# Weight maxima reduced by TensorE in place of GpSimd, and the first two turns of a fused recurrent kernel in another order

## What is computed

```
xn = layernorm(x)                       # over the 128 channels
# layer 0
xm = xn * time_mix + shift(xn) * (1 - time_mix)
k, v, r = exp(min(xm @ Wk.T, 60)), xm @ Wv.T, xm @ Wr.T
wkv, wk = causal_conv(k * v, w), causal_conv(k, w) + 1e-9   # w: exponential decay + a factor for the present
s = (sigmoid(r) * wkv / wk) @ Wo.T
h = relu(s0 * [xn, -xn] @ sign(k0)) * 2;  h = relu(s1 * h @ sign(k1)) * 2;  g = silu(s2 * h @ sign(k2))
x = x + s * g
# layer 1: a state-space block for s, a mixture of 2 shared and 16 routed experts for g
x = x + s * g
```

## Time and profile before

| | us |
|---|---|
| median of three runs (lowest, highest) | 738.07 (735.55, 738.98) |
| the profiled execution | 734.49 |
| its span | 732.7 |
| TensorE busy in the span | 642.5 (88%) |
| VectorE busy | 635.7 (87%) |
| ScalarE busy | 509.4 (70%) |
| GpSimd busy | 281.5 (38%) |

### The profile page before, as it was taken

One profiled execution on the slowest core, in us unless ns is written; L12 is line 12 of the kernel. 1 busy time (PEld: TensorE's weight loads), 2 busy tenths in 40 slices (PEclk: granted clock), 3 DMA queues, 4 the chain that ended last, 5 costly groups with the idle time before them and its releaser, 6 DMA issues. The chain is left out here.

```text
span 732.7 us, 10841 instructions
## 1 busy us (share of the span) xinstructions
PE 642.5 (88%) x2711; PEld 304.7 (42%) x2711; DVE 635.7 (87%) x1467; ACT 509.4 (70%) x800; POOL 281.5 (38%) x278
## 2 busy tenths in 40 slices
PE   2795899999999985598999899999999999999986
PEld 1342444444444442343444444444444444544432
DVE  4996999999999997758988988988898898889766
ACT  2463566766666652687877887787788779788775
POOL 6456666777767762031222123032212303221220
PEclk9898999999999997899999999999999999999999
DMA  5420000000000000000000000000000000000000
GB/s 151 110 90 26 0 0 0 0 0 0 0 0 0 1 0 1 0 1 0 15 1 15 15 0 14 14 14 0 14 14 0 14 14 14 0 14 14 1 16 29
DMA packets 10739, 11.29 MB, mean 15 GB/s; under 512 B 4800, under 2 KB 6288, under 8 KB 10720
## 3 DMA queue, kind: packets, MB, share of 16 engines
q1 hardware_dynamic: 9744, 10.73, 4.8%
q0 software_dynamic: 112, 0.33, 0.2%
q10 hardware_dynamic: 864, 0.00, 0.1%
HBM read 6.87 MB, written 4.19 MB: 15 GB/s over the span
## 5 line engine op out<-in xcount | busy, mean ns | idle before, releaser
L1058 PE MATMUL bank<-arena,w 128*128 128x512 f16 x640 | 153.9, 389 | 20.0 <-DVE arena L717 14.1
L1058 PE MATMUL bank<-arena,dnT 128*128 128x512 f32 x288 | 138.6, 592 | 0.0
L613 ACT ACTIVATE arena<-bank,xinv 128x512 f32<-128x512 f32 x144 | 95.6, 687 | 51.0 <-PE bank L1058 50.8
L443 POOL TENSOR_TENSOR arena<-arena 128x512 f32<-128x512 f32 x48 | 59.7, 1271 | 151.8 <-ACT arena L550 151.8
L1058 PEld LDWEIGHTS bank<-arena,w 128*128 128x128 f16 x640 | 63.4, 100 | 99.0 <-issue 24.5
L476 ACT ACTIVATE arena<-bank 128x512 f16<-128x512 f32 x96 | 53.9, 606 | 35.1 <-PE bank L1058 35.1
L433 POOL TENSOR_TENSOR arena<-arena 128x512 f32<-128x512 f32 x16 | 17.1, 1067 | 150.5 <-DVE arena L917 150.5
L1058 PE MATMUL bank<-arena,wsqT 128*128 128x512 f32 x128 | 65.6, 617 | 6.0 <-DVE arena L726 6.0
L1058 PEld LDWEIGHTS bank<-arena,dnT 128*128 128x128 f32 x288 | 53.7, 191 | 36.0 <-issue 24.3
L926 DVE SCALAR_TENSOR_TENSOR arena<-bank,cws,arena 128x506 f32<-128x506 f32 (+1 forms) x96 | 67.1, 740 | 1.1
L717 DVE SCALAR_TENSOR_TENSOR arena<-bank,arena 128x512 f16<-128x512 f32 x96 | 60.2, 670 | 1.7 <-ACT arena L476 0.5
(11 more groups left out here) (208 smaller groups left out, 1525.3 us busy)
## 6 DMA issues: line engine op xcount, KB each, us to landing
x_all<-in_L_attn_x SPq DMA_DIRECT2D x16, 256.0 KB, 2.7
out<-x_all SPq DMA_DIRECT2D x16, 256.0 KB, 2.0
up_n<-in_L_ffn_routed_up SPq DMA_DIRECT2D x1, 512.0 KB, 3.8
dn_n<-in_L_ffn_routed_down SPq DMA_DIRECT2D x1, 512.0 KB, 5.4
wx<-in_L_attn_W_x SPq DMA_DIRECT2D x1, 288.0 KB, 2.8
k_u<-in_L_ffn_k POOLq DMA_DIRECT2D x1, 256.0 KB, 5.1
w_in<-in_L_attn_W_in SPq DMA_DIRECT2D x1, 256.0 KB, 2.4
k_u<-in_L_ffn_k SPq DMA_DIRECT2D x1, 128.0 KB, 5.7
```

Of the source, the lines that this page charges most:

```text
L443: g.tensor_tensor(prod[:, c, :], act[:, c + 1, :], gate[:, :], ALU.mult).then_inc(sem["b_actp"], 1)
L613: a.activation(act[:, c, :], q_U[(c + 1) % 2][:, :], ACT.Gelu, scale=xinv[:, I_UP:I_UP + 1]).then_inc(sem["b_act"], 1)
L1058: return nc.tensor.matmul(ps, lhsT, rhs, start=start, stop=stop)
```

## The change

Seven edits, all in the stretch ahead of turn 3:

1. `partition_all_reduce` on POOL is gone. In turn 1, PE transposes `amax` into the bank `b_S`, DVE takes the maximum of each of the 7 rows and multiplies the identity by it (`largest`, between its two scans), PE multiplies ones by that diagonal matrix, which puts the seven maxima into every partition, and DVE copies them back after its four low parts. PE's first s product waits for that copy.
2. `scales` runs after turn 1 in place of after turn 2.
3. Group 0's rows are normalised by DVE (four instructions) and no longer by POOL (two).
4. DVE forms `w0` and the sign constants after `xm` of turn 0, and the decays after the four low parts of turn 0, which now stand ahead of the scans. ACT's four high parts of turn 0 stand behind the exponential, and its small constants behind `xh`.
5. The turned squares are made in two halves (two banks), and ACT takes them out.
6. PE waits for Wk and Wv alone before its first work; k0 is loaded third, Wr and Wo behind it, each with a semaphore of its own. ACT's small loads have three semaphores in place of one.
7. POOL's clearing of buffers comes two instructions earlier, and with it SyncE's loads of layer 1's weights.

```diff
-            for i in range(4):
-                last = nc.tensor.transpose(b_S[:, i * P:(i + 1) * P], wsq[:, i, :], ident[:, :])
-            last.then_inc(sem["square_turned"], 1)
+            def square_turned(half):
+                for i in range(2):
+                    last = nc.tensor.transpose((b_S, b_F)[half][:, i * P:(i + 1) * P], wsq[:, 2 * half + i, :], ident[:, :])
+                last.then_inc(sem["square_turned"], 1)
+            square_turned(0)
...
-            def constants():
-                pool.wait_ge(sem["absmax_ready"], NSC)
-                g.partition_all_reduce(amax[:, :], amax[:, :], P, bass.bass_isa.ReduceOp.max).then_inc(sem["absmax_all"], 1)
-            bodies(pool, layer0, {1: constants, G - 1: lambda: spread_of_rows(0)})
+            bodies(pool, layer0, {G - 1: lambda: spread_of_rows(0, "b_")})
...
-            normalise(0, "a_")
+            spread_of_rows(0, "a_")
...
+                if isinstance(f, int) and f == 1:
+                    pe.wait_ge(sem["absmax_ready"], NSC)
+                    pe.wait_ge(sem["square_ready"], 1)
+                    nc.tensor.transpose(b_S[0:NSC, 0:P], amax[:, :], ident[:, :]).then_inc(sem["absmax_turned"], 1)
...
+                if isinstance(f, int) and f == 1:
+                    pe.wait_ge(sem["absmax_diag"], 1)
+                    mm(b_S[:, P:P + NSC], ones[0:NSC, :], adiag[0:NSC, :]).then_inc(sem["absmax_spread"], 1)
...
+                    if isinstance(m, int) and m == 0:
+                        pe.wait_ge(sem["absmax_all"], 1)
...
+            normalised(0, "a_")
...
+            def largest():
+                dve.wait_ge(sem["absmax_turned"], 1)
+                link(v.tensor_reduce(amx[0:NSC, :], b_S[0:NSC, 0:P], AX.X, ALU.max))
+                v.tensor_scalar(adiag[0:NSC, :], ident[0:NSC, 0:NSC], amx[0:NSC, 0:1], None,
+                                ALU.mult).then_inc(sem["absmax_diag"], 1)
...
+                if isinstance(f, int) and f == 1:
+                    dve.wait_ge(sem["absmax_spread"], 1)
+                    v.tensor_copy(amax[:, :], b_S[:, P:P + NSC]).then_inc(sem["absmax_all"], 1)
...
-            bodies(dve, layer0, {0: magnitudes, 2: scales, G - 1: matrices, G: turned_matrices})
+            bodies(dve, layer0, {0: magnitudes, 1: scales, G - 1: matrices, G: turned_matrices})
```

More of the change, by code:

```diff
@@ L495, in layer0 @@
                     high(1, m, 2)
+                if isinstance(f, int) and f == 0:
+                    for j in range(FC):
+                        high(0, 0, j)
                 if has(f):
@@ L507, in layer0 @@
                     a.activation(thr[:, :], b_RX[:, :], ACT.Tanh, scale=0.5).then_inc(sem["a_thr"], 1)
-                    high(0, f, 0)
+                    if not (isinstance(f, int) and f == 0):
+                        high(0, f, 0)
                     actv.wait_ge(sem["a_thr"], f + 1)
@@ L511, in layer0 @@
                     a.activation(sr[:, :], thr[:, :], ACT.Copy, scale=0.5, bias=0.5).then_inc(sem["a_sr"], 1)
-                    high(0, f, 1)
-                    high(0, f, 2)
-                    high(0, f, 3)
+                    if not (isinstance(f, int) and f == 0):
+                        high(0, f, 1)
+                        high(0, f, 2)
+                        high(0, f, 3)
                 if has(m):
@@ L712, in _, with normalised @@
-            v.tensor_scalar(c3[:, 2:3], c3[:, 1:2], 0.5, None, ALU.mult).then_inc(sem["const_done"], 1)
+            def normalised(n, ph):
+                dve.wait_ge(sem[ph + "rstd"], n + 1)
+                after(dve, sem[ph + "xnT"], n)
+                for j in range(J):
+                    last = v.tensor_scalar(xn[:, j, :], x_all[:, bass.ds(n * N + j * P, P)], mv[:, j, 0:1],
+                                           rstd[:, j:j + 1], ALU.subtract, ALU.mult)
+                last.then_inc(sem[ph + "xn"], 1)
@@ L714, in low, with decays @@
+            def decays():
+                dve.wait_ge(sem["const_ready"], 7)
+                dve.wait_ge(sem["chan_ready"], 3)
+                dve.wait_ge(sem["const_done"], 1)
+                v.tensor_scalar(c3[:, 2:3], c3[:, 1:2], 0.5, None, ALU.mult)
+                v.tensor_scalar(dec[:, 0:P], ones[:, :], tch[:, 1:2], None, ALU.mult)
+                v.tensor_scalar(dec[:, P:T], ones[:, 0:T - P], tch[:, 1:2], None, ALU.mult).then_inc(sem["const_done"], 1)
             def low(layer, n, j):
@@ L751, in layer0 @@
                     v.tensor_tensor(kv[:, :], ekm[:, :], b_V[:, :], ALU.mult).then_inc(sem["a_kv"], 1)
+                if isinstance(f, int) and f == 0:
+                    for j in range(FC):
+                        low(0, 0, j)
+                    decays()
+                    dve.wait_ge(sem["const_done"], 2)
                 if has(m):
@@ L884, in turned_low @@
                 v.scalar_tensor_tensor((xl, xl_)[par][:, :], ps[:, :], XS, (xh, xh_)[par][:, :], ALU.mult, ALU.subtract).then_inc(sem["b_xl"], 1)
-            def normalised(n):
-                dve.wait_ge(sem["b_rstd"], n + 1)
-                after(dve, sem["b_xnT"], n)
-                for j in range(J):
-                    last = v.tensor_scalar(xn[:, j, :], x_all[:, bass.ds(n * N + j * P, P)], mv[:, j, 0:1],
-                                           rstd[:, j:j + 1], ALU.subtract, ALU.mult)
-                last.then_inc(sem["b_xn"], 1)
-            bodies(dve, layer0, {0: magnitudes, 2: scales, G - 1: matrices, G: turned_matrices})
+            bodies(dve, layer0, {0: magnitudes, 1: scales, G - 1: matrices, G: turned_matrices})
             def top_four(n):
@@ L1110, in layer0 @@
                     turn_rows(b_T).then_inc(sem["a_xnT"], 1)
+                if isinstance(f, int) and f == 0:
+                    pe.wait_ge(sem["wr_loaded"], WR_ALL)
+                    square_turned(1)
                 if has(m):
```

110 lines of the change are left out of this document (66 added, 44 removed).

## The result

The changed kernel took 729.02 us (median of four runs, 724.93 to 730.5) against 738.04 for the kernel before beside it (four runs, 735.55 to 738.98): the medians differ by 9.0 us. The ratio on record is 0.9896, with a 95% interval of 0.9867 to 0.9925, which is a gain of 7.7 us, between 5.5 and 9.8. Forecast were 726.3 and a gain of 11.8: faster, as predicted and inside the range, but by less. The profiled executions are 734.49 and 728.02, 6.5 apart; 722.7 was forecast for the second.

A forecast was written before the change was run, and what follows sets the result against it. DVE fills the loop turns; POOL's 13.33 us absence for the reduction lengthens turn 2 to 3. X = 26.6 + 15.45 + 3.5 = 45.6; gain 57.35 - 45.6 = 11.8, so 738.07 becomes 726.3 us (profiled 722.7), range 722.5 to 731.5.

The forecast's parts named there:

- The rule of the Trainium skill: At POOL's reduction: only the first call's code loading of some 6 us counts, nothing behind it; gain 4.9 us.
- D: Loop turns 2 to 14: scans beside POOL's products add 1.1 to 1.3 us per turn; 743.3 at most; chance 0.03.
- Turn 0: Start of layer 0: `xm` of turn 0 at 10.4 us, then 16.2 to `xm` of turn 1, at 26.6.
- the normalising: Ahead of `xm` of turn 0: DVE's four normalising instructions take 1.6 us, bounds 1.11 and 2.78.
- the term of turn 1: From `xm` of turn 1 to the end of `sg`: 15.45 us, where before took 16.19.
- rival B: Turn 1: PE's clock falls after idle time; k, v and two hidden blocks slow, 2.0 us less gain, 728.3; chance 0.20.
- `largest`: DVE in turn 1: the row reduction and 7x7 product take 0.5 us for both, ends 0.3 and 1.9.
- `scales`: In its new place after turn 1: 3.5 us, ends 2.4 and 5.57.
- C: Ends of turn 1 and start of turn 2: PE's waits also lower the clock; with B some 4 us more, 732.3; chance 0.10.
- each of the two waits is below 2 us: Argument against C: PE's waits in turn 1 for the diagonal and for the copy are each below 2 us.
- The rest of the kernel only moves earlier: Behind turn 4: everything keeps its length, so the gain of 11.8 us carries to the end.
- the steps apply from X on: From the start of turn 2's `xm`, X = 45.6 us: the before's steps of 15.15 and 15.53 follow to turn 4.

The follow-up runs named there:

- e7: The kernel before with the POOL reduction done twice in a row; 734.32 us (one run) against 734.09 for before.
- e1: The kernel before with edits 1 and 2 alone, its start left as before; 729.71 us against 735.47, ratio 0.9914.
- e6: The changed kernel with `scales` back after turn 2, the reduction staying on TensorE; 731.26 us (one run) against 734.09 for before.
- e4: The changed kernel with 18 overwritten products in PE's idle time ahead of k and v of turn 1; 724.36 us, ratio 0.9832 to before.
- e8: The changed kernel with POOL's two large normalising steps for group 2 behind its three products of turn 1; 725.68 us (one run) against 734.09 for before.
- e5: The changed kernel with the edits of e3 and e4 together; 724.02 us against 734.09 for before, ratio 0.9847.
- e3: The changed kernel with DVE's copy of the maxima ahead of the four low parts of turn 1; 728.03 us, ratio 0.9873 to before.
- e12: The changed kernel with the edits of e4 and e8, plus 34 overwritten products in PE's idle time between the layers; 722.41 us, ratio 0.9848 to before.
- e2: The changed kernel with the reduction back on POOL and `scales` back after turn 2; 735.08 us against 735.47 for before, ratio 0.9991.
- e9: e1 with 20 overwritten products in PE's idle time before turn 1's first hidden products; 726.72 us against 735.04 for before, ratio 0.9874.

## Why the prediction was right, and where it was wrong

**Right: what bounds and what goes.** POOL's absence of 13.33 us was the cause of the long step; without the reduction PE's 5.87 and DVE's 6.91 are gone (they stand again in e7), and by e1 the whole measured gain comes from edits 1 and 2. Which share is whose isn't shown: without edit 2 the lead at turn 4 was 3.1 (e6). The rule of the Trainium skill, GPSIMD Engine Reference, section Instruction dispatch, by itself (gain 4.9) was rightly set aside: e7 shows both idle times as a pair, and at T4 e1 gained 8.97, with the 1 us of scatter. The loop's pace is unchanged (15.53), so D, the slower rival, did not occur. Turn 0 was nearly right: 10.80 for 10.4, and 16.41 for 16.2 to turn 1. In it the normalising took 1.62 for 1.6, and neither of the bounds, 1.11 and 2.78, was near.

**Wrong: the term of turn 1.** From `xm` to the end of `sg` 15.45 were forecast, and 45.92 - 27.21 = 18.71 measured up to the start of `scales`. The 3.26 us more fall, step by step by the start times of DVE, into:

- 1.00 at the low parts (34.07 to 36.41, where 37.35 to 38.69 before): k and v at the lower clock. This is rival B, in which the forecast had put 0.20. B was priced at 2.0; e4 shows 2.65 at T4. It came in a smaller form than described: k and v lost 1.80, and the 16 hidden products behind them nothing (3.65).
- 0.80 and 0.97 at the two pairs of scans. The prediction asked for POOL's contention in turn 0 and, with D, in the loop, but took the scans of turn 1 over from before, where they had ended just as POOL began. `largest` between the pairs puts the second one onto POOL's work (e1, e4), the wait ahead of them also the first. e8, with POOL's order alone changed, brings both back.
- 0.35 at `largest` (0.85 for 0.5, inside the bounds of 0.3 and 1.9), and 0.39 at the end: s took 1.10 and came later behind the copy, so DVE waited 0.77, not 0.33. Small terms give 0.25 back.

**Wrong, and in its favour: `scales`.** 3.5 were forecast, with 2.4 as the lower end; it took 1.95, with all 16 instructions at 0.12 to 0.23. The lower end, 5.57 less four times 0.8, took off too little. e5 and e6 show the same list at 3.52 and 4.46 as soon as POOL works beside it.

**C came in part.** Behind the wait of 2.44 us ahead of s the granted clock fell (0.50 from 46 to 48), and the next 8 hidden products took 3.38. That is the 16.15 us step from turn 2 to 3 where 15.15 was taken over from before: 1.00 more. Against it stood "each of the two waits is below 2 us"; one was longer. C's price of 4 was too high; e3, in which this wait is gone, has the full clock there and a step of 15.10.

**Not in the sum: what comes behind.** "The rest of the kernel only moves earlier" was wrong. 8.49 us at T4 became 6.58 at the second normalised rows of layer 1 (307.15 - 300.57) and 6.5 at the end of the profiled pair. That the start of layer 1 can meet a lower clock wasn't thought of. Whether it does so because it comes earlier, or for something in this stretch, stays open: e12 wins 2.2 us there ahead of the `w_in` products and leaves these at the lower clock, so it doesn't show why nine unlike kernels fall in the same group.

**How the number came inside the range.** In part by errors that cancel. `xm` of turn 2 came 2.3 late: 0.6 from the start and 3.3 from turn 1, less 1.6 won in `scales`. The step to turn 3 added 1.0 and the stretch between the layers 1.9, together 5.2 of the 5.3 us by which the profiled execution, 728.02, missed 722.7. The range held the median of 729.02 because it had been drawn wide enough for B.

**Edits costed at nothing.** Edits 3 to 7 are worth 2.9 to 3.2 us at turn 0 and 1.4 at turn 1. At turn 4 they are worth 2.3 where the reduction stays on POOL (e2 against before), but -0.5 (e1 against after) or 0.4 (e9 against e4) with edits 1 and 2, nothing beside the scatter. That they would be kept was the unspoken part of "the steps apply from X on"; in the changed kernel PE stands still for 3.95 us ahead of k and v, with its clock down behind it, and with PE kept busy in both most of the lead goes all the same: where it goes then wasn't followed.

## What to carry to other kernels

In this kernel a custom instruction of GpSimd of 0.40 us kept its engine away for 13.33. Such a one is priced by how long the engine is away, ahead of it and behind it, and then by who waits for what it owed next. When such an absence is taken out, look again at what its engine now does in that time, since VectorE's scans and tiny instructions beside it can double or grow fivefold and more, and at where TensorE now stands idle, since it is slower behind that. Remedies of this kind hold for one timing: three that each came 1.0 to 2.7 us earlier at turn 4 alone came 0.6 earlier together, no more than the scatter.

## What the runs showed of the hardware beyond that

- A VectorE instruction on 7x7 values took 0.22 to 1.14 us, and one on 128x1 values 0.12 to 1.22 (1.74 for one in turn 0 of the changed kernel); the long ones lay beside GpSimd's work. A pair of scans of 128x256 took 1.24 to 3.18 (e2).
- The time of one kernel follows TensorE's mean granted clock from run to run. Four runs of the changed kernel gave 724.93 at 0.985, 728.02 at 0.975, 730.02 and 730.5 at 0.971. That is as large as most of the effects here. T4 scatters by about 1 us, so it tells the experiments apart somewhat better than a single time does, and not below that. The Trainium skill, TensorE: Matmul & The Clock Gate, section What's actually happening, says that the number of products at the lower clock differs from run to run of one kernel and puts the cost of the ramp under 1% of a typical span. That it differs agrees: 6.49 and 5.30 us for the same 16 products in before and e7. The 5.6 us between these runs are 0.8%, but they are a difference between runs and not the whole cost, which no run here shows.
- The length of the idle time doesn't tell which products, or how many, run at the lower clock behind it. After 3.95 or 3.96 us, with the same list of PE, k and v and the 16 hidden products behind them took 3.68 and 3.65 us in the changed kernel, 3.78 and 4.29 in e3, and 2.56 and 4.78 in e8.
- Work that nobody reads can make a kernel faster. 18 products in a gap of PE won 2.65 us at T4, and the median of that kernel is 3.7 below e3's on the same chip, which lacks them and has the copy earlier.
